# Ranking eight experts: the ranks of two scoring stages are added up by TensorE in PSUM from seven comparisons of VectorE, in place of a chain on VectorE

## What is computed

```python
# layer 0
probs = softmax(hidden @ router_w.T)                     # (tokens, 8)
sampled_k = argmax(clip(actor_logits, -30, 30)) + 1      # 1..6, one per token
order = argsort(-probs); rank = argsort(order)
scores = where(rank < sampled_k, probs, 0)
out = sum over e of scores[e] * expert_e(hidden)         # then x + tanh(g_ffn[0]) * out
# layer 1
probs = softmax(x @ Wg)
top_w, top_i = top_k(probs, 2); top_w = top_w / (sum(top_w) + 1e-8)
out = sum over the two experts of top_w * expert(x)      # then x + tanh(g_ffn[1]) * out
```

## Time and profile before

| what | value |
|---|---|
| runs, median (lowest to highest) | 2243.23 us (2242.27 to 2245.75) |
| profiled execution, own time | 2245.57 us |
| its span | 2243.7 us, 82073 instructions |
| TensorE matmul busy | 2083.9 us, 93% |
| VectorE busy | 1932.0 us, 86% |
| ScalarE busy | 1553.9 us, 69% |
| GpSimd busy | 1599.4 us, 71% |
| mean granted clock of TensorE | 0.966 of full |
| DMA | 121.39 MB, 54 GB/s over the span |

### The profile page before, as it was taken

One profiled execution on the slowest core, in us unless ns is written; L12 is line 12 of the kernel. 1 busy time (PEld: TensorE's weight loads), 2 busy tenths in 40 slices (PEclk: granted clock), 3 DMA queues, 4 the chain that ended last, 5 costly groups with the idle time before them and its releaser, 6 DMA issues. The chain is left out here.

```text
span 2243.7 us, 82073 instructions
## 1 busy us (share of the span) xinstructions
PE 2083.9 (93%) x28022; PEld 1634.7 (73%) x28022; DVE 1932.0 (86%) x4355; ACT 1553.9 (69%) x3446; POOL 1599.4 (71%) x1521
## 2 busy tenths in 40 slices
PE   3999999975999999999995999999999964999999
PEld 2788888843666666666664999999999962666666
DVE  5899999986888888888885888888888878888888
ACT  3788888863555555555563777777777755888887
POOL 1577777632666666666665999999999942888887
PEclk9999999976999999999997999999999987999999
DMA  5000000003322232222321455555455430000000
GB/s 156 9 6 6 6 6 6 7 1 78 99 89 79 83 89 76 86 84 78 89 65 36 78 80 80 80 78 77 77 77 77 78 71 1 11 14 14 9 14 14
DMA packets 476586, 121.39 MB, mean 54 GB/s; under 512 B 432023, under 2 KB 446999, under 8 KB 475748
## 3 DMA queue, kind: packets, MB, share of 16 engines
q1 hardware_dynamic: 344132, 86.86, 18.3%
q10 hardware_dynamic: 132384, 33.63, 6.6%
HBM read 106.51 MB, written 13.89 MB: 54 GB/s over the span
## 5 line engine op out<-in xcount | busy, mean ns | idle before, releaser
L1164 POOL TENSOR_TENSOR f_low<-f_hidden,f_high 128x512 f16<-128x512 f32 x336 | 442.4, 1322 | 217.7 <-ACT f_high L1096 215.9
L1122 DVE TENSOR_TENSOR f_hidden<-f_hidden,f_share 128x512 f32<-128x512 f32 x336 | 374.6, 1115 | 0.0
L1311 POOL TENSOR_TENSOR f_low<-f_hidden,f_high 128x512 f16<-128x512 f32 x256 | 296.9, 1161 | 82.9 <-ACT f_high L1254 82.6
L1102 ACT ACTIVATE f_act_out<-f_gate 128x512 f32<-128x512 f32 x336 | 200.6, 597 | 192.5 <-PE f_gate L1066 192.5
L1145 DVE SCALAR_TENSOR_TENSOR f_hidden<-f_up,f_act_out 128x512 f32<-128x512 f32 x336 | 229.8, 684 | 82.8 <-PE f_up L1066 50.9
L1687 POOL TENSOR_TENSOR a_q_head_high<-a_q_t_high,a_head_mask 128x2048 f16<-128x2048 f16 x64 | 233.0, 3641 | 55.7 <-PE a_score L1489 47.5
L1096 ACT ACTIVATE f_high<-f_hidden 128x512 f16<-128x512 f32 x336 | 210.8, 627 | 73.0 <-DVE f_hidden L1122 71.6
L1076 PE MATMUL f_y<-w_high,f_high 128*128 128x128 f16 x1344 | 243.4, 220 | 2.0 <-POOL f_low L1164 2.0
L1076 PE MATMUL f_y<-w_low,f_high 128*128 128x128 f16 x1344 | 243.4, 220 | 0.0
L1076 PE MATMUL f_y<-w_high,f_low 128*128 128x128 f16 x1344 | 243.4, 220 | 0.0
L1687 POOL TENSOR_TENSOR a_q_head_low<-a_q_t_low,a_head_mask 128x2048 f16<-128x2048 f16 x64 | 232.9, 3639 | 0.0
(11 more groups left out here) (263 smaller groups left out, 8525.2 us busy)
## 6 DMA issues: line engine op xcount, KB each, us to landing
f_share<-expert_shares SPq DMA_DIRECT2D x128, 256.0 KB, 3.2
a_q_pos<-queries ACTq DMA_DIRECT2D x64, 512.0 KB, 3.9
f_share<-expert_shares SPq DMA_DIRECT2D x128, 128.0 KB, 3.0
relative_values<-a_rel_all SPq DMA_DIRECT2D x512, 8.0 KB, 1.7
x_all<-in_x SPq DMA_DIRECT2D x4, 1024.0 KB, 8.1
f_share<-expert_shares SPq DMA_DIRECT2D x128, 32.0 KB, 1.8
queries<-a_q_parts SPq DMA_DIRECT2D x64, 64.0 KB, 4.1
a_rel<-relative_values SPq DMA_DIRECT2D x64, 64.0 KB, 3.3
```

What stands on the lines that cost most here:

```text
L1102: nc.scalar.activation(act_out[m % RING][:, :], gate_ps[m % BANKS][:, :], ACT.Silu, scale=1.0 / WSCALE).then_inc(act_ready, 1)
L1122: nc.vector.tensor_tensor(hidden[r][:, :], hidden[r][:, :], share[k][:, :, :].rearrange("p t q -> p (t q)"), ALU.mult).then_inc(scaled, 1)
L1164: nc.gpsimd.tensor_tensor(low[r][:, :], hidden[r][:, :], high[r][:, :], ALU.subtract).then_inc(low_ready, 1)
L1311: nc.gpsimd.tensor_tensor(low[k][:, :], hidden[k][:, :], high[k][:, :], ALU.subtract).then_inc(low_ready, 1)
```

## The change

The ranks are no longer kept on VectorE. Each comparison is made on the shifted logits (before their exponential) and written as 0 or 1 in bfloat16 to a tile of its own; it depends on no other comparison. TensorE adds them up in one PSUM bank: with an identity matrix `plus` and its negative `minus` as weights, it adds `after`, subtracts each comparison from the front experts, adds it to the back ones, and in e0 adds minus the allowed number. VectorE then reads the bank once: rank below zero (e0) or below two (e1), times the share, is one instruction. In e0 the actor's instructions stand between the comparisons. The gate multiplies the 128 x 64 reciprocals and no longer the 128 x 512 shares. All tiles of shares are laid out expert by expert, so the logits are read with a stride of 8 values, the sums over experts with a stride of 64, and `scores` in e1 is written with a stride of 8. ACT makes `plus`, `minus` and the widened `after_all`, ahead of the exponential. In e1 the load of `first` is gone; the six loads in e0 stand where they stood.

```diff
-                sp.wait_ge(consts_in, 32)
...
+                nc.scalar.activation(plus[:, :], ident[:, :], ACT.Copy).then_inc(consts_ready, 1)
+                nc.scalar.activation(minus[:, :], ident[:, :], ACT.Copy, scale=-1.0).then_inc(consts_ready, 1)
+                act.wait_ge(after_in, 16)
+                nc.scalar.activation(after_all[:, :, :], after[:, :].unsqueeze(2).broadcast_to([P, NE, B]),
+                                     ACT.Copy).then_inc(consts_ready, 1)
                 act.wait_ge(step, 2)
-                nc.scalar.activation(probs[:, :, :], probs[:, :, :], ACT.Exp).then_inc(exped, 1)
+                nc.scalar.activation(share[:, :, :], shifted[:, :, :], ACT.Exp).then_inc(exped, 1)
...
+                pe.wait_ge(consts_ready, 3)
+                nc.tensor.matmul(rank_ps[:, :], plus[:, :], flat(after_all), start=True, stop=False, skip_group_check=True)
+                for d in range(1, NE):
+                    pe.wait_ge(compared, d)
+                    nc.tensor.matmul(rank_ps[:, 0:(NE - d) * B], minus[:, :], flat(not_less[d]), start=False, stop=False,
+                                     skip_group_check=True)
+                    mm = nc.tensor.matmul(rank_ps[:, d * B:NE * B], plus[:, :], flat(not_less[d]), start=False,
+                                          stop=(actor is None and d == NE - 1), skip_group_check=True)
+                if actor is not None:
+                    pe.wait_ge(allowed_ready, 1)
+                    for e in range(NE):
+                        mm = nc.tensor.matmul(rank_ps[:, e * B:(e + 1) * B], plus[:, :], minus_allowed[:, :], start=False,
+                                              stop=(e == NE - 1), skip_group_check=True)
+                mm.then_inc(ranked, 1)
...
+                def compare(d):
+                    nc.vector.tensor_tensor(not_less[d][:, :, :], shifted[:, 0:NE - d, :], shifted[:, d:NE, :],
+                                            ALU.is_ge).then_inc(compared, 1)
...
-                link(nc.vector.tensor_copy(rank[:, :, :], after[:, :].unsqueeze(1).broadcast_to([P, B, NE])))
-                for d in range(1, NE):
-                    ge, front, back = cmp_[:, :, 0:NE - d], slice(0, NE - d), slice(d, NE)
-                    link(nc.vector.tensor_tensor(ge, probs[:, :, front], probs[:, :, back], ALU.is_ge))
-                    link(nc.vector.tensor_tensor(rank[:, :, front], rank[:, :, front], ge, ALU.subtract))
-                    link(nc.vector.tensor_tensor(rank[:, :, back], rank[:, :, back], ge, ALU.add))
-                link(nc.vector.tensor_tensor(rank[:, :, :], rank[:, :, :], wide(allowed), ALU.is_lt))
-                link(nc.vector.tensor_tensor(probs[:, :, :], probs[:, :, :], rank[:, :, :], ALU.mult))
...
+                dve.wait_ge(step, done)
+                dve.wait_ge(ranked, 1)
+                rank3 = rank_ps[:, :].rearrange("q (e n) -> q e n", e=NE)
+                if s_dram is not None:
+                    nc.vector.scalar_tensor_tensor(out=by_expert[:, :, :], in0=rank3, scalar=0.0, in1=share[:, :, :],
+                                                   op0=ALU.is_lt, op1=ALU.mult).then_inc(scores_ready, 1)
```

More of the change, by code:

```diff
@@ L881, in _, with expert_scores, sb, sem @@
                     tanh(s)
-def expert_scores(nc, name, B, io, logits, actor, scores, gate, ident=None, s_dram=None, loads=(), loads_in=None):
+def expert_scores(nc, name, B, io, logits, actor, scores, gate, ident, s_dram=None, loads=(), loads_in=None):
     with ExitStack() as ctx:
[L889 to L895, removed]
+        def sb(n, s, d=F32):
+            return ctx.enter_context(nc.sbuf_tensor(f"{name}_{n}", s, d))
+        def sem(n):
+            return ctx.enter_context(nc.semaphore(f"{name}_{n}"))
+        shifted, share = sb("shifted", [P, NE, B]), sb("share", [P, NE, B])
+        not_less = [None] + [sb(f"not_less{d}", [P, NE - d, B], BF16) for d in range(1, NE)]
+        after, after_all = sb("after", [P, NE]), sb("after_all", [P, NE, B], BF16)
+        plus, minus = sb("plus", [P, P], BF16), sb("minus", [P, P], BF16)
+        top, total, inverse = sb("top", [P, B]), sb("total", [P, B]), sb("inverse", [P, B])
+        rank_ps = ctx.enter_context(nc.psum_tensor(f"{name}_rank_ps", [P, NE * B], F32))
+        after_in, consts_ready = sem("after_in"), sem("consts_ready")
+        step, exped, compared, ranked = sem("step"), sem("exped"), sem("compared"), sem("ranked")
+        if actor is not None:
+            first, allowed, best = sb("first", [P, MAX_K]), sb("allowed", [P, B]), sb("best", [P, B])
+            minus_allowed = sb("minus_allowed", [P, B], BF16)
+            first_in, choice, allowed_ready = sem("first_in"), sem("choice"), sem("allowed_ready")
         if s_dram is not None:
@@ L982, in _ @@
[L982 to L987 removed]
+                    nc.vector.tensor_scalar(a3, a3, 30.0, -30.0, ALU.min, ALU.max).then_inc(choice, 1)
@@ new lines, in _ @@
+                dve.wait_ge(step, 1)
+                nc.vector.tensor_tensor(shifted[:, :, :], logits[:, :, :].rearrange("q g (t e) -> q e (g t)", e=NE), each(top),
+                                        ALU.subtract).then_inc(step, 1)
+                if actor is not None:
+                    dve.wait_ge(choice, 1)
+                    nc.vector.tensor_reduce(best[:, :], a3, AX_X, ALU.max).then_inc(choice, 1)
+                dve.wait_ge(step, 2)
+                compare(1)
+                compare(2)
@@ new lines, in _ @@
+                dve.wait_ge(exped, 1)
+                nc.vector.tensor_reduce(total[:, :], by_token(share), AX_X, ALU.add).then_inc(step, 1)
+                dve.wait_ge(step, 3)
+                nc.vector.reciprocal(inverse[:, :], total[:, :]).then_inc(step, 1)
+                dve.wait_ge(step, 4)
+                if s_dram is not None:
+                    nc.vector.tensor_scalar(inverse[:, :], inverse[:, :], gate, None, ALU.mult).then_inc(step, 1)
+                    dve.wait_ge(step, 5)
```

103 lines of the change are left out of this document (56 added, 47 removed).

## The result

The changed kernel takes 2223.39 us, the median of four runs (2221.73 to 2225.18), beside 2244.0 us (2242.27 to 2245.75) for the kernel before on the same chip: a ratio of 0.9908, 95% interval 0.9891 to 0.9925, or 20.6 us less. The forecast was 2223.0 us in 2218.5 to 2228.5. The total was right; two of its terms were not, with opposite signs.

A forecast was written before the change was run, and what follows sets the result against it. Both scorings were taken to be bound by a VectorE chain with all else idle; gains of 10.75 us in e0 and 9.44 in e1, together 20.2, off the median of 2243.23 gave 2223.0 us, range 2218.5 to 2228.5.

The forecast's parts named there:

- The bound: Both scorings: a VectorE chain with all else idle, so each us taken off moves all that follows forward by one.
- Length plus 0.03 with a wait, less 0.09 without: VectorE in both scorings: an instruction's cost in us, by whether it waits for its predecessor; chains of 8.8 and 9.3 us.
- The rule against it: VectorE in both scorings: the Trainium skill's claim that leaving out semaphores gains nothing; +1.7 us, 2224.7.
- I take zero: Six VectorE instructions of 512 values with a stride in SBUF: the stride was taken to cost nothing.
- rival A: Both scorings: strided SBUF operands slow six VectorE instructions by some 0.5 us each, 3.0 us, 2226.0; chance 8%.
- ACT late in e1, by 0.3 us: Second scoring: copy and table load of 1.28 us delay ACT's exponential to 1878.05; VectorE waits 0.3 us.
- TensorE hidden by 1 us in e0: First scoring: TensorE's rank matmuls end by 522.4, and VectorE asks for the ranks at 523.46.
- nearly a tie: Second scoring: TensorE's ranks are ready at 1879.8, and VectorE asks for them at 1880.07.
- rival C: Starts of f0 and f1: new matmuls get TensorE's full clock granted and kept, gaining 3.9 us more, 2219.1; chance 10%.
- The loads of tables: First scoring: six loads stay hidden before f0, with cover of 3.8 us or more in place of 14.
- D: f0: an earlier start locks its tiles into a slower rhythm, eating the gain, 2247.7 or more; chance 1%.
- E: Both scorings: their time is hidden after all and the change does nothing; chance 2%.

The follow-up runs named there:

- experiment 3: Changed kernel with a wait put back behind each VectorE instruction that had none, 15 in e0 and 7 in e1: 2228.23 us.
- experiment 6: Changed kernel with ACT's table loaded early, exponentials also written token by token for flat sums, and e1's first division dropped: 2221.72 us.
- experiment 8: Changed kernel plus shorter chain, spare matmuls and GpSimd fills replacing the `after` load: 2220.67 us; beside it the unaltered changed kernel again: 2224.6 us.
- experiment 9: Changed kernel with 14 waited spare products in e0, so f0 starts when it did before: 2234.55 us; also the kernel before again: 2243.82 us.

## Why the prediction was right, and where it was not

- **The bound.** This was right. Both scorings were bare chains of VectorE, and all of the 18.3 us taken off them is passed on: the experts' stages start 4.6 and 0.3 us behind the chains, where it was 4.7 and 0.55. Either scoring alone shows its own chain shorter and the other's unchanged, and 10.1 us of padding in e0 brought the time up by 10.0 to 11.2.
- **Length plus 0.03 with a wait, less 0.09 without.** This was right for what it was taken for: flat operands give 8.78 and 9.38 us for the forecast's 8.8 and 9.3. Two comparisons and their successor are 1.00 us apart, as its 0.53 and 0.47 say. The rule against it fell with experiment 3. Its price of 1.7 us was too low by the forecast's own numbers: from less 0.09 to plus 0.03 is 0.12 for each of 22 instructions, 2.3 us after the 0.3 that hides. The waits cost 2.9.
- **"I take zero" for strided operands.** This term failed. The six instructions take 1.06, 1.03, 1.07, 1.03, 1.03 and 1.08 us, 6.30 for 6 x 0.69 = 4.14, so 2.2 us, 72% of the bound of 3.0. Of it 0.3 replaces the wait for the exponential, and 1.9 lengthens the chains: forecast gain 20.2, measured 18.3. The failed step was to let a row of PSUM decide over SBUF. One row of SBUF did speak: line 983 writes with a stride at 0.66 for the flat 0.49 of line 987. The forecast put that down to "the pace of any two-input instruction", but line 983 reads only one tile, like line 987. By that row alone the six strides would have been 6 x 0.17 = 1.0 us; rival A had too small a chance at 8%.
- **ACT late in e1, by 0.3 us.** This was right, 0.22 with flat operands; in the changed kernel the strided subtraction hid it.
- **TensorE hidden by 1 us in e0, "nearly a tie" in e1.** This was right in kind: the slack was 1.9 and 0.8 us, larger in part since the stride made VectorE later. In experiment 6 the tie turned into a wait of 1.43 us.
- **The clock, rival C.** In the changed kernel it stayed at 0.50 until 3.7 us into f0 (4.7 in the change's second profile; 5.0 and 3.4 in two profiles of the kernel before). Where it rose within e0 by itself, it fell before f0. Where it was made to stay, it gave 1.6 us in the timeline and not 3.9: 2.45 of C's price was counted in f0, where ACT's copy and table load hold the first tile, not TensorE. f1 gave 1.1 of its 1.45, and 0.46 came from the transposes, which C did not have.
- **The loads of tables.** This was right: no wait for a load shows. The cover was larger than the forecast's bounds of 14 and 3.8 us: the DMA engines are quiet from 522.0 on in both kernels, 17.6 us ahead of f0 before and 8.0 now.
- **D and E.** f0 kept its rhythm. Its length is 665.0 us here, 666.3 in the change's second profile, and 665.0 in the kernel before's second; over all fourteen profiles it is 665.0 to 666.9, a scatter of 1.9 us.
- **What the forecast did not have:** 2.5 us in the stretch with the attention of layer 1, which made up for the strides, and 0.3 us at the ends of the two stages. 18.3 + 0.3 + 2.5 = 21.1 us, against 20.6 between the medians. The second pair of medians, in experiment 8, gives 19.2. That the number 2223.0 was so near is luck: two misses of 1.9 and 2.5 us cancelled.

## What to carry to other kernels

Where a stage is one engine's chain with the rest idle, price the chain instruction by instruction; with flat operands, the kind that its rows showed, the sum here held to 0.1 us. A layout that makes one operand flat makes another strided: price that stride by a row of the same memory and of the same kind of instruction, and put it on the engine with time to spare, here ACT. After taking the chain down, look for the next in line at once: here it was TensorE at half clock, which starts behind a 4 KB load. The shorter chain, the spare matmuls, the table loaded early and a fill on the idle GpSimd in place of that load gave 3.9 us more together; what each gave was not all measured apart.

## What was not expected of the hardware

- 512 values of 4 bytes at a stride of 8 or 64 values in SBUF take VectorE 1.03 to 1.08 us for 0.69, and 512 values at a stride of 64 take ACT 1.08 for 0.63. In PSUM the stride shows no price: line 1035 of experiment 6 reads the ranks with a stride of 64 at 0.69.
- Independent VectorE instructions follow each other 0.13 to 0.15 us sooner than waited ones (experiment 3), where the forecast had 0.12.
- A load of 4 KB was there 1.5 to 2.0 us after its issue in 25 of 26 cases, and once 3.1 us after it, which cost that chain over 1 us.
- The same few matmuls in e0 met a granted clock of 0.50 in one execution and of 1.00 in another (experiment 9). It changed no chain, since VectorE was the later one.
- A full granted clock helps where TensorE is what is waited for, and only there: 1.1 us in f1, and in f0 0.1 us beside the change's first profile, 0.6 at most beside its second.
